# The first stage of a one-core kernel: float32r products, one weight product made beforehand, and rows normalised by ScalarE

## The reference, cut to what matters

```python
xn = _layernorm(x, axis=-1)                       # rows of 256
x, z = jnp.split(jnp.einsum('tbd,de->tbe', h, W_xz), 2, axis=-1)
dt = jax.nn.softplus(jnp.einsum('tbd,de->tbe', x, W_dt) + b_dt)
Bm = jnp.einsum('tbd,dn->tbn', h, W_B)            # n = 16
Cm = jnp.einsum('tbd,dn->tbn', h, W_C)
...
inp = (dt * x)[..., None] * Bm[:, :, None, :]
```

## Time and profile before

| | |
|---|---|
| median of 3 runs | 4025.93 us (4025.74 to 4030.18) |
| span of the profiled execution | 4055.7 us (no other time is recorded for it; 29.8 us above the median of the runs) |
| busy, whole span | PE 84%, DVE 79%, ACT 59%, POOL 32% |
| granted TensorE clock, mean | 0.920 |
| first stage | the first 249.58 us of the span |

### The profile page before, as it was taken

How to read it: one execution, slowest core, us unless ns; L and a number is a source line. 1 busy time by engine, 2 the same in 40 slices (tenths; PEclk the granted TensorE clock), 3 DMA queues, 4 the chain that set the end, 5 groups by cost and what they waited for, 6 DMA issues and landing times. The chain is left out here.

```text
span 4055.7 us, 64760 instructions
## 1 busy us (share of the span) xinstructions
PE 3421.6 (84%) x19475; PEld 2015.0 (50%) x19476; DVE 3205.1 (79%) x4243; ACT 2410.3 (59%) x4320; POOL 1304.2 (32%) x905
## 2 busy tenths in 40 slices
PE   8968989987559799897999999999999964389950
PEld 3445555554448689795333333333333322189950
DVE  8959999998876466467899999999999923378768
ACT  6768888885964433210577777777777750133323
POOL 4439989986014444301000000000000006644520
PEclk9979999998889899997799999999999986699975
DMA  6664444444859733395122323232232124223258
GB/s 213 251 210 168 162 157 160 163 158 148 278 180 251 201 89 92 91 291 143 26 53 61 68 55 73 53 72 57 57 71 52 31 70 126 83 81 91 89 168 294
DMA packets 531451, 521.08 MB, mean 128 GB/s; under 512 B 84784, under 2 KB 441264, under 8 KB 531040
## 3 DMA queue, kind: packets, MB, share of 16 engines
q1 hardware_dynamic: 517248, 480.45, 40.3%
q0 software_dynamic: 13952, 37.74, 2.7%
HBM read 301.15 MB, written 215.71 MB: 127 GB/s over the span
## 5 line engine op out<-in xcount | busy, mean ns | idle before, releaser
L2315 DVE TENSOR_REDUCE at_top<-at_psM 128x1 f32<-128x1024 f32 x1024 | 1205.6, 1219 | 101.2 <-PE at_psM L2174 99.8
L2283 ACT ACTIVATE at_probs<-at_psS 128x512 f32<-128x512 f32 x2048 | 1061.0, 603 | 286.3 <-PE at_psS L2200 286.3
L2200 PE MATMUL at_psS<-at_q,at_k 64*128 64x512 f32 x2048 | 803.6, 471 | 8.2 <-ACT at_probs L2283 8.2
L2174 PE MATMUL at_psM<-at_k,at_q 62*128 62x512 f32 x2048 | 705.2, 454 | 41.4 <-DMA at_vraw<-scratch_vf 21.9
L575 POOL TENSOR_TENSOR sc_prod<-sc_state,sc_c_row 128x1024 f32<-128x1024 f32 x256 | 648.7, 2564 | 84.7 <-DVE sc_state L726 72.6
L2174 PEld LDWEIGHTS at_psM<-at_k,at_q 62*128 62x128 f32 x2048 | 312.9, 190 | 621.6 <-DVE at_top L2315 539.6
L726 DVE TENSOR_TENSOR_SCAN sc_state<-sc_dec,sc_psI 128x1024 f32<-128x1024 f32 x256 | 574.3, 2276 | 43.7 <-PE sc_psI L647 34.0
L2213 PE MATMUL at_psV<-at_probs,at_v 128*32 128x512 f32 x4096 | 546.3, 605 | 0.0
L658 PE MATMUL sc_psY<-sc_prod,sc_ident 128*128 128x512 f32 x1024 | 480.4, 599 | 15.3 <-DVE sc_y L712 15.3
L2200 PEld LDWEIGHTS at_psS<-at_q,at_k 64*128 64x128 f32 x2048 | 337.7, 184 | 170.3 <-ACT at_probs L2283 160.5
L2141 POOL COPY at_v<-at_vraw 128x256 f32<-128x256 f32 x32 | 12.8, 401 | 1250.4 <-DMA at_vraw<-scratch_vf 1167.5
(11 more groups left out here) (398 smaller groups left out, 4928.7 us busy)
## 6 DMA issues: line engine op xcount, KB each, us to landing
sc_c_row<-scratch_bc SPq DMA_DIRECT2D x128, 512.0 KB, 3.7
scratch_xs<-at_zeros SPq DMA_DIRECT2D x140, 264.0 KB, 4.7
sc_b_row<-scratch_bc SPq DMA_DIRECT2D x32, 512.0 KB, 5.0
ec_y<-scratch_ys SPq DMA_DIRECT2D x32, 512.0 KB, 6.1
ex_x<-scratch_xs SPq DMA_DIRECT2D x39, 264.0 KB, 2.8
si_x<-in_x SPq DMA_DIRECT2D x16, 512.0 KB, 4.4
scratch_xn<-si_xn SPq DMA_DIRECT2D x16, 512.0 KB, 5.1
scratch_x_t<-si_xT SPq DMA_DIRECT2D x16, 512.0 KB, 5.7
```

Source lines behind the costliest of these rows:

```text
L2174: ins = pe.matmul(psM[t % 2][:, half * TILE:(half + 1) * TILE], rows_of(q4[j], h, 0, MAXROW)[:, c * P:(c + 1) * P], rows_of(k4[j], h, 0, M ...
L2200: pe.matmul(psS[v % 3][:], rows_of(k4[j], h, 0, GROUP)[:, c * P:(c + 1) * P], rows_of(q4[j], h, 0, GROUP)[:, half * TILE:(half + 1) * TILE ...
L2283: act.activation(probs[:, slot(j, v), :], psS[v % 3][:], ACT.Exp).then_inc(act_done, 1)
L2315: dve.tensor_reduce(top[j % 2][:, h, c:c + 1], psM[t % 2][:], AX.X, ALU.max, negate=True).then_inc(maxed, 1)
```

## The change

The first stage is rewritten:

- Each float32 product becomes three float32r products of two-part operands: an operand a is split into a head (rounded to float32r) and a rest (a minus head), and head*head, rest*head and head*rest are summed in PSUM. Heads are copies by ScalarE, rests are subtractions by VectorE (`rest`). Weights are split once, before the first tile.
- The matrix W_x W_dt is made once, before the first tile (`wd_p`), and dt's product starts from `xn` and no longer from `xT`. It stays in `psD`; the W_B, W_C product moves to `psX` after `xT` has been copied out.
- Rows are normalised by ScalarE (`activation` with scale `rstd` and bias `shift`), and GpSimd makes `shift` = -mean * rstd in two more small instructions per tile.
- softplus is `max(v, ln(1 + min(exp(v), 1e13)))`: ScalarE passes twice, both from one table loaded at the start; VectorE caps the exponential (`cap`) and takes the maximum straight from `psD`.
- `uT` = dt * x moves from VectorE to GpSimd (`product`).
- `x` has three buffers; no loop, all 16 tiles are written out.

```diff
             @block.gpsimd
+                def product(i):
+                    pool.wait_ge(dt_ready, i + 1)
+                    free(pool, u_st, i)
+                    pool.tensor_tensor(uT[i % 2][:], dtT[i % 2][:], xT[i % 2][:], ALU.mult).then_inc(u_ready, 1)
+                for i in range(NT):
+                    if i:
+                        product(i - 1)
+                    if i + 3 < NT:
+                        deviation(i + 3)
+                    if i + 1 < NT:
+                        rounding(i + 1)
...
             @block.vector
+                def rest(i):
+                    dve.wait_ge(head_ready, i + 1)
+                    dve.wait_ge(xb_ready, i + 1)
+                    later(dve, dt_psum, i - 1)
+                    dve.tensor_tensor(xp[i % 2][1][:], psT[:], xp[i % 2][0][:].bitcast(F32), ALU.subtract).then_inc(rest_ready, 1)
+                def cap(i):
+
+                    dve.wait_ge(e_ready, H * i + H)
+                    dve.tensor_scalar(e[:], e[:], EXP_CAP, None, ALU.min).then_inc(cap_ready, 1)
...
-                    dve.scalar_tensor_tensor(out=dtT[par][:], in0=vb[:], scalar=0.0, in1=soft[:],
-                                             op0=ALU.max, op1=ALU.add).then_inc(dt_ready, 1)
-                    dve.tensor_tensor(uT[par][:], dtT[par][:], xT[par][:], ALU.mult).then_inc(u_ready, 1)
+                    for h in range(H):
+                        ins = dve.scalar_tensor_tensor(out=dtT[i % 2][:, h, :], in0=psD[:, h, :], scalar=bdt[:, h:h + 1],
+                                                       in1=soft[:, h, :], op0=ALU.add, op1=ALU.max)
+                    ins.then_inc(dt_ready, 1)
...
             @block.scalar
+                act.preload_act_table_set("natural_log_exp_and_others")
+                        ins = act.activation(xn[i % 2][:, s, :], x[i % 3][:, s, :], ACT.Identity,
+                                             bias=shift[i % 2][:, s:s + 1], scale=rstd[i % 2][:, s:s + 1])
+                    act.activation(xp[i % 2][0][:], psT[:], ACT.Copy).then_inc(head_ready, 1)
+                        act.activation(e[:, h, :], psD[:, h, :], ACT.Exp, bias=bdt[:, h:h + 1]).then_inc(e_ready, 1)
+                    act.activation(soft[:], e[:], ACT.Ln, bias=1.0).then_inc(soft_ready, 1)
...
             @block.tensor
+                        (wh, wl), (xh, xl) = (weight(part, k) for part in two), (xp[i % 2][part][:, k, :] for part in two)
+                        last = products(pe, dst, ((wh, xh), (wl, xh), (wh, xl)), k == 0, k == H - 1)
+                for i in range(NT):
+                    pe.wait_ge(rest_ready, i + 1)
+                    later(pe, bc_ready, i)
+                    for h in range(H):
+                        last = project(psX[:, h, :], lambda part, k: wxz_p[part][:, k, h * P:(h + 1) * P], i)
+                    last.then_inc(x_psum, 1)
+                    if i + 1 < NT:
+                        transposes(i + 1)
...
```

More of the change, by code:

```diff
@@ L191, in ssm_inputs, with rows, later, free @@
             [m.sem(f"{n}_st{k}") for k in two] for n in ("xn", "x", "z", "bc", "dt", "u", "xq"))
-        x_in = A["x"].rearrange("(i s p) d -> i p s d", p=P, s=SUB)
-        xn_out = A["xn0"].rearrange("(i s p) d -> i p s d", p=P, s=SUB)
+        def rows(name, i):
+            return A[name].rearrange("(i s p) d -> i p s d", p=P, s=SUB)[i, :, :, :]
         def tile(name, i):
             return A[name].rearrange("h p (i t) -> i p h t", t=TILE)[i, :, :, :]
[L198 to L213, removed]
+        def later(eng, sem, value):
+            if value > 0:
+                eng.wait_ge(sem, value)
+        def free(eng, sems, i):
+            later(eng, sems[i % 2], 16 * (i // 2))
         with nc.Block() as block:
@@ L226, in rows_out @@
-                def rows_out(i, par, then_load):
+                    sp.dma_start(tile(name, i), buf[i % 2][:]).then_inc(sems[i % 2], 16)
+                def rows_out(i):
                     sp.wait_ge(xn_ready, i + 1)
                     m.settle(sp)
[L229 to L237, removed]
+                    if i + 3 < NT:
+                        load(i + 3)
+                    sp.dma_start(rows("xn0", i), xn[i % 2][:]).then_inc(xn_st[i % 2], 16)
@@ L249, in _ @@
[L249 to L256, removed]
@@ L339, in step @@
[L339 to L343, removed]
+                    free(dve, dt_st, i)
+                    later(dve, u_ready, i - 1)
+                    for h in range(H):
+                        ins = dve.scalar_tensor_tensor(out=dtT[i % 2][:, h, :], in0=psD[:, h, :], scalar=bdt[:, h:h + 1],
+                                                       in1=soft[:, h, :], op0=ALU.add, op1=ALU.max)
@@ new lines, in _ @@
+                maxima(0)
+                step8(0)
+                for i in range(NT):
+                    if i:
+                        cap(i - 1)
+                    if i + 1 < NT:
+                        maxima(i + 1)
+                    x_out(i)
+                    if i:
+                        dt_part(i - 1)
+                    if i + 1 < NT:
+                        rest(i + 1)
+                    if i + 3 < NT:
+                        variance(i + 3)
+                    if i + 1 < NT:
+                        step8(i + 1)
+                    bc_out(i)
@@ L402, in _, with transposes @@
+                exponential(NT - 1)
+                logarithm(NT - 1)
             @block.tensor
             def _(pe):
[L404 removed]
+                def transposes(i):
                     pe.wait_ge(xn_ready, i + 1)
[L406 to L408 removed]
+                    later(pe, rest_ready, i)
+                    later(pe, xb_ready, i)
                     for s in range(SUB):
@@ L444, in _ @@
-                transposes(0, 0)
-                pe.wait_ge(weights, 80)
-                turns(pe, step)
 def ssm_scan(nc, A):
```

295 lines of the change are left out of this document (169 added, 126 removed).

## The result

| | before | after |
|---|---|---|
| median | 4028.05 us (4 runs, 4025.74 to 4031.09) | 3990.65 us (4 runs, 3988.61 to 3994.82) |
| ratio, 95% interval | | 0.9912 [0.9900, 0.9924] |
| span of the profiled execution | 4055.7 | 3988.9 |
| granted clock, mean | 0.920 | 0.922 |
| last `uT` of the first stage ends | 245.14 | 207.52 |

The change makes the kernel 37.4 us faster; 3994 was forecast, within 3979 to 4008. The two spans differ by 66.8 us, which is 29.4 more than the runs: the profiled execution of before spent about 30 us more in the routing stage, far behind the change. The first stage ends 37.4 us earlier, and that is all of the measured gain.

The account below looks back on a forecast made before the run. VectorE was taken to bound the first stage, TensorE close behind. After: 16.4 + 14.5 + 142.8 (twelve tiles at 11.9) + 22.1 + 17.1 = 212.9 against 245.14, 32.2 less: 3994 us, range 3979 to 4008.

Parts of the forecast that it names:

- What bounded before: First stage: VectorE's step of 13.77 us sets the pace, TensorE's 13.21 close behind; relieving one alone would win little.
- The normalisations: VectorE before the change: four last 5.45 us together, the first ending about with `si_r`, the last with `si_xq`.
- TensorE, 10.74: TensorE per tile after the change: 42 products at 0.235 us plus 0.87 for transposes.
- The ring with the cap: VectorE and GpSimd, each tile: cap waits until `si_r` ends at 5.2, then 6.77 of VectorE work; 11.9 us per tile.
- My first rival: Cap on VectorE does not wait for `si_r`; TensorE bounds at 11.1 us per tile, 3984 in all; chance 0.20.
- my forecast: Cap waits for `si_r` in every tile, 11.9 us per tile, 3994 us in all; chance 0.48.
- Small instructions of GpSimd: Four before `si_r` take 2.1 us, so `si_r` starts 2.75 after VectorE's `AGGREGATE` starts.
- Start and end: First stage: first product at 16.4 us, first tile 14.5, last two steady tiles 11.4 and 10.7, last tile 17.1.
- The other prices: Per tile: ScalarE 8.6 us with normalisations of 0.52 each, GpSimd about 9.7; stores at a share of 0.81 cost nothing.
- The half clock: Rival: TensorE idle ahead of `psX` drops to 1.2 GHz, up to 9.6 us more per tile, 4128 at worst; chance 0.05.

Follow-up runs that it names:

- the one-port cap: Changed kernel with the cap as a three-operand instruction whose unused second input is in PSUM: 3984.38 us; run again, 3984.09 against 3990.12 for the changed kernel.
- the rounding first: Changed kernel with GpSimd's order swapped, `si_r` and `si_xq` ahead of the four small instructions of the deviation: 4045.42 us, 1.0047 of before.

## Why the prediction was right

**What bounded before.** The normalisations were read one place off: taken singly in the trace, the first lasts 0.41 and goes ahead of `si_r`, and it is the second that ends with `si_r` (48.80) and the fourth that ends with `si_xq`. No sum hangs on that. What bounded was VectorE by 0.5 and TensorE close behind, so that relief of one alone would win little. The runs confirm it for one side: with TensorE's records of before, the whole rest of the change ends the stage 7.3 us earlier, and the other 30.1 (242.24 against 212.16) come with TensorE's products. For the other side there are only parts. `uT` alone back on VectorE costs 9.7 of the 37, the normalisations alone 11.5. With all of VectorE's relief taken back everything is lost, and more, but that run doesn't show this cause by itself: GpSimd's new order and the half clock are in it. The weight product made beforehand, the third buffer and the written-out tiles weren't run by themselves.

**TensorE, 10.74.** It is 10.97. Products start 2.87/12 = 0.239 apart instead of 0.235 (the six of W_B, W_C 0.232), 0.13 in a tile; the transposes take 0.79 instead of 0.87; and from `psD` to the next `psX` it is 3.04 (119.00 to 122.04), 0.17 more than between other groups, which I had at nothing.

**The ring with the cap.** This was the forecast's core, and it is right in kind: the cap waits for `si_r` to its end, TensorE then waits for `si_bc`, a tile takes 12.08, where 11.9 was worked out. The term that was off is its count. I let it happen in all tiles; it happens in every other one. A tile that VectorE delayed has `psX` waiting for it, so TensorE is early in VectorE's next step: `psD` is done at 109.91, 1.25 behind `AGGREGATE` (108.66), the exponential is early, the cap wins (111.25 against 112.27). That tile is TensorE's, VectorE waits 1.08 at `xT` (114.14), and now `psD` is done 2.35 behind `AGGREGATE` (121.96 against 119.61), and the cap loses. My first rival (no wait, 0.20) and my forecast (0.48) were both true, tile by tile. I had seen that 0.25 us decide and treated the race as one outcome. That 3994 came so close to 3990.65 is in part luck: the mean of 11.53 lies between the two outcomes, and 12.08 in all tiles would have been some 7 us more (six tiles, 1.1 each).

**Small instructions of GpSimd.** 2.1 from start to `si_r` was too low: `si_r` starts 3.1 to 3.6 behind `AGGREGATE`, not 2.75. `ve` takes 0.58 here, against 0.23 in the earlier trace rows. The rows show why: it ends at 109.70 and the fp8 step on VectorE at 109.61; the next ends at 110.42 and that step's second half at 110.34; `rstd` takes 1.58 when a cap runs beside it (ends 111.98 and 111.94) and 1.03 at 121.36, without one. Without the cap, and with the one-port cap, `rstd` takes 1.03 in every tile of the steady part, and with the rounding first, where no fp8 step runs beside it, `ve` takes 0.23. So GpSimd waits for VectorE's instructions too. I counted that only one way. The Trainium skill (SBUF — State Buffer, Who interferes with whom) says that the order of issue decides who waits. The rows of `ve` agree (the fp8 step started 0.17 before it). Those of `rstd` don't, by their starts: it began at 110.40, 0.85 ahead of the cap, and still ended with it; and of the two caps 0.26 behind `si_r` above one waited and one won. The starts in the trace don't settle who was first. The one-port cap (1.22 beside a running `si_r`) agrees with the section's rule on instructions with one SBUF input.

**Start and end.** First product at 17.48 for 16.4, the first tile 12.42 for 14.5 (twelve products took 4.35, not 5.6), the fourteen tiles behind it 160.61 for 164.9, the last 17.01 for 17.1. Together 207.52 for 212.9: 5.4 us, about as much as the forecast gain of 32.2 was short of 37.4. Of it 1.1 more at the start and 2.1 less in the first tile partly cancel.

**The other prices.** ScalarE: 70% of 11.53 is 8.1 against 8.6; the normalisation takes 0.59, not 0.52. GpSimd: 85% is 9.85 against 9.7. Stores cost nothing at a share of 0.86, as said. The half clock didn't appear in the steady part of the change (1.00 from 40 to 190 us), only in its first tile (0.50 from 17 to 20 us). It did appear where VectorE's relief was taken back, after 6.3 us of idle time, and with the rounding first, where TensorE had waited 2.37 and 2.33 in one tile and the next twelve products took 4.57 (0.50 from 126 to 128 us). The rival was real, its condition wasn't met.

## What to carry to other kernels

When two engines are within 4% of each other, price the kernel with each half of the change alone: here the relief of VectorE alone was worth 4 to 7 us, that of TensorE alone could win little as long as VectorE had no hole (so the rows say; it wasn't run by itself), and both together gave 37. A wait between two instructions that race by a fraction of a microsecond isn't a yes or no: follow two steps in a row, since the outcome of one sets the start of the next. And where an instruction of VectorE waits for one of GpSimd, look for a form that reads one input from SBUF before you move it in the order; nearly twice as long without the wait was 6 us better, while one swap on an engine with 15% to spare cost 55.

## What the runs showed of the hardware

- Instructions of VectorE and GpSimd that run side by side can hold up either: `si_e` 0.69 alone and 2.33 behind `si_r`, `ve` 0.23 alone and 0.58 behind an fp8 step, `rstd` 1.03 and 1.58 (2.47 in the run with the normalisation on VectorE).
- Thirty-one table loads more, 1.28 each, ended the first stage 2.0 us later; the exponential started 0.04 after a load's end.
- A float32r product of 512 columns with its weight load takes 0.24; a float32 one is two records, 0.86 (3.44 for four).
- After 6.3 us of idle time TensorE's granted clock was 0.50 and twelve products took 5.46; after 1.2 us, in the change, it stayed at 1.00 and they took 3.03.
